# A chain of four transformer blocks on one core: setup as turns beside the first tiles, norms that overlap the last tile's end, one product a scan step, 102-column mixes

## What is computed

```python
# block 0 (8 heads of 32)
x = x + mha(layernorm(x), layernorm(ctx))          # softmax(q k / sqrt(32)) v, then W_o
U = (layernorm(x) @ W_in.T + b_in) @ Bmat          # 64 numbers a row
s = 0
for t in range(1024):                              # a recurrence over the rows
    s = silu(s @ A.T) + U[t]; states[t] = s
x = x + states @ Cmat + (ctxb.mean(axis=1) @ W_prog.T + b_prog)
# block 1 (16 heads of 64), keys and values from layernorm(ctx), causal mask
x = mha(layernorm(x)) @ wo + bo + x
# block 2 (16 heads of 16), mask, then a layernorm over the sum
e = exp(scores - max) * mask; probs = e / (e.sum() + 1e-9)
x = layernorm((probs @ v) @ Wo.T + bo + x) * ln_g + ln_b
# block 3 (16 heads of 16), mask, and an MLP of 1024
x = x + mha(layernorm(x)) @ proj_w + proj_b
x = x + gelu(layernorm(x) @ fc1_w + fc1_b) @ fc2_w + fc2_b
```

## Time and profile before

| | us |
|---|---|
| median of 3 runs | 1478.64 |
| lowest, highest | 1478.23, 1479.79 |
| profiled execution | 1479.49 |
| its span, first to last instruction | 1477.7 |
| TensorE busy, of the span | 1387.4 (94%) |
| VectorE, ScalarE, GpSimd busy | 932.8, 670.1, 559.6 |
| mean granted clock of TensorE | 0.995 of 2.4 GHz |

### The profile page before, as it was taken

One profiled execution on the slowest core, in us unless ns is written; L12 is line 12 of the kernel. 1 busy time (PEld: TensorE's weight loads), 2 busy tenths in 40 slices (PEclk: granted clock), 3 DMA queues, 4 the chain that ended last, 5 costly groups with the idle time before them and its releaser, 6 DMA issues.

```text
span 1477.7 us, 22985 instructions
## 1 busy us (share of the span) xinstructions
PE 1387.4 (94%) x8827; PEld 1147.8 (78%) x8827; DVE 932.8 (63%) x2180; ACT 670.1 (45%) x1483; POOL 559.6 (38%) x699
## 2 busy tenths in 40 slices
PE   6899989999899999999999999989998999899999
PEld 5777777877688678878787887768876887798778
DVE  4677773177755776486757546776577467737771
ACT  3565665513454354534453442335434634453344
POOL 4245342022731463345235411174137314621561
PEclk8999999999999999999999999999999999999999
DMA  4122322020000000000000000000000000000000
GB/s 96 59 61 80 100 94 93 0 84 5 1 8 21 2 2 15 15 1 8 8 15 1 8 16 15 3 1 8 22 1 1 15 15 1 1 15 15 1 1 15
DMA packets 46729, 34.09 MB, mean 23 GB/s; under 512 B 21980, under 2 KB 45339, under 8 KB 46107
## 3 DMA queue, kind: packets, MB, share of 16 engines
q1 hardware_dynamic: 46571, 32.59, 7.8%
q10 hardware_dynamic: 48, 0.01, 0.0%
HBM read 23.26 MB, written 8.39 MB: 21 GB/s over the span
## 4 chain that ended last, share of the span: by engine, by line
PE 76%; DVE 7%; issue 6%; POOL 5%; ACT 3%; DMA 1%; SPq 0%; ACTq 0%; DVEq 0%; POOLq 0%
PE ps L803 11%; PE ps L795 9%; PE ps L755 8%; PE ps L842 8%; PE ps L851 8%; PE ps L774 7%; PE ps L765 6%; PE ps L727 5%; PE ps L811 5%; PE ps L713 4%; PE ps L945 1%; DVE mx L1247 1%; DVE zt L1222 1%; POOL pr L1497 1%; POOL pr L1511 1%
## 5 line engine op out<-in xcount | busy, mean ns | idle before, releaser
L1472 POOL TENSOR_TENSOR rstd<-mv,halfneg 128x1 f32<-128x1 f32 x192 | 106.6, 557 | 501.8 <-DVE mv L1214 500.7
L1511 POOL TENSOR_TENSOR pr<-mx,pr 128x616 f32<-128x616 f32 x128 | 156.2, 1220 | 212.9 <-DVE mx L1247 212.1
L1066 ACT ACTIVATE pr<-pr 128x616 f32<-128x616 f32 x224 | 159.5, 715 | 155.9 <-POOL pr L1511 89.0
L1070 ACT ACTIVATE pr<-ps 128x512 f32<-128x512 f32 x224 | 132.6, 596 | 184.6 <-PE ps L774 183.6
L803 PEld LDWEIGHTS ps<-vtab,pr 128*128 128x128 f32 (+1 forms) x1280 | 165.6, 192 | 21.8 <-ACT pr L1070 17.7
L803 PE MATMUL ps<-vtab,pr 128*128 128x102 f32 (+2 forms) x1280 | 175.3, 285 | 7.0 <-ACT pr L1070 3.5
L1311 DVE TENSOR_TENSOR xt<-xt,ps 128x256 f32<-128x256 f32 x192 | 80.2, 418 | 157.8 <-PE ps L851 70.3
L774 PE MATMUL ps<-ident,pr 128*128 128x128 f32 (+1 forms) x1120 | 160.0, 276 | 13.5 <-POOL pr L1497 5.9
L774 PEld LDWEIGHTS ps<-ident,pr 128*128 128x128 f32 (+1 forms) x1120 | 125.1, 139 | 43.2 <-ACT pr L1066 14.2
L1045 ACT ACTIVATE tt<-ps 128x256 f32<-128x256 f32 x160 | 61.0, 382 | 202.8 <-PE ps L713 202.5
L795 PE MATMUL ps<-vwo,pr 128*128 128x256 f32 (+1 forms) x640 | 149.5, 382 | 1.1 <-ACT pr L1070 0.8
(11 more groups left out here) (198 smaller groups left out, 2406.4 us busy)
## 6 DMA issues: line engine op xcount, KB each, us to landing
out_dram<-xt SPq DMA_DIRECT2D x64, 128.0 KB, 1.7
xt<-in_x_dram SPq DMA_DIRECT2D x32, 128.0 KB, 2.2
xt<-out_dram SPq DMA_DIRECT2D x32, 128.0 KB, 2.1
fc<-in_L_xattn_fc_w_dram SPq DMA_DIRECT2D x2, 1024.0 KB, 7.5
wk<-in_L_xattn_wkv_dram SPq DMA_DIRECT2D x1, 2048.0 KB, 10.0
front<-in_L_xattn_wkv_dram SPq DMA_DIRECT2D x1, 2048.0 KB, 7.7
wo<-in_L_xattn_wo_dram SPq DMA_DIRECT2D x1, 1024.0 KB, 5.2
kb<-in_L_xattn_wq_dram SPq DMA_DIRECT2D x1, 1024.0 KB, 5.0
```

Source lines behind the costliest of these rows:

```text
L1066: ac(v, v, ACT.Exp, scale=-ATTN[key[0]].scale).then_inc(done["expo"], 1)
L1070: ac(pr[:, run.lane, 0:4 * P], bank(run.lane, 0), ACT.Copy).then_inc(done["pturn_main"], 1)
L1472: p.tensor_tensor(rstd[:, lane:lane + 1], mv[:, lane, 1:2], halfneg[:, :], ALU.pow).then_inc(done["rstd"], 1)
L1511: p.tensor_tensor(p8, mx[:, run.lane, :].unsqueeze(2).to_broadcast([P, HG, KEYS]), p8, ALU.subtract).then_inc(done["below"], 1)
```

## The change

It has four parts.

1. **Setup's items are a plan "i"** with turns on every engine, on four banks (4 to 7, of lanes 2 and 3) instead of eight, so that the first tiles' steps stand among them. The query weights come first, then the packed vectors. All `w0` copies are on ScalarE. Six of the twelve DMAs of block 0's values are issued by ScalarE, the others by SyncE. SyncE loads the first tiles of x between the weights, and the fc2 weights wait for the last query of phase 0.
2. **The next tile's start overlaps the last one's end.** In phase 0 its norm stands ahead of the output product, its turn and query after the residual add, its bias before `uproj`; it has buffers of its own (`z0`, `t0`, in the memory of the fc2 weights), statistics of its own, and bank 1. In phase 1 its load, state product (now in bank 1), resume and statistics stand ahead of the last tile's second half of fc2. All strings of `TURNS` are new.
3. **The scan has one product a step.** `sums` holds silu plus `U`; VectorE adds it after each silu (`carry`). `R` becomes two small buffers. `states` and its adds are gone.
4. **Mixes of blocks 2 and 3** stream two copies of three heads, 102 columns instead of 153.

```diff
-COPIES, WCOPY = 3, 160
+COPIES, WCOPY = (3, 2), 160
...
+def lane_steps(lane):
+    first, second = runs_of(lane)[:RUNS], runs_of(lane)[RUNS:]
+    out = [(s, k, first[0]) for s, k in FIRST_NORM + FIRST_QUERY + FIRST_BIAS]
+    for n, run in enumerate(first):
+        follow = first[n + 1:n + 2]
+        out += [(s, k, run) for s, k in FIRST_HEADS]
+        out += [(s, k, f) for f in follow for s, k in FIRST_NORM]
+        out += [(s, k, run) for s, k in FIRST_PROJ]
+        out += [(s, k, f) for f in follow for s, k in FIRST_QUERY]
+        out += [(s, k, run) for s, k in FIRST_STATE]
+        out += [(s, k, f) for f in follow for s, k in FIRST_BIAS]
+        out += [(s, k, run) for s, k in FIRST_U]
+    for n, run in enumerate(second):
+        follow = [] if n + 1 in (RUNS // 2, RUNS) else [second[n + 1]]
+        if n in (0, RUNS // 2):
+            out += [(s, k, run) for s, k in SECOND_GET + SECOND_SSM + SECOND_NORM]
+        out += [(s, k, run) for s, k in SECOND_MAIN]
+        out += [(s, k, f) for f in follow for s, k in SECOND_GET + SECOND_SSM]
+        out += [(s, k, run) for s, k in SECOND_END]
+        out += [(s, k, f) for f in follow for s, k in SECOND_NORM]
+    return out
...
-        steps += [("scan_u", n), ("scan_r", n), ("silu", n)]
+        steps += [("scan_mm", n), ("silu", n), ("carry", n)]
...
+ITEMS = [("w0", i) for i in range(4)] + [("pack", 0)] + [("zT", kc) for kc in range(KC)] + [("w0", 4), ("w0", 5)]
+ITEM_BANKS = (4, 5, 6, 7)
...
             def turn(key, run):
-                        pe.wait_ge(done["u_sb"], at("u_sb", "u", prev(run)))
+                        pe.wait_ge(done["resid"], at("resid", "0", prev(run)))
...
             def scores(key, run):
+                        if run.no > RUNS:
+                            pe.wait_ge(done["resid"], at("resid", "m", prev(run)))
...
+                    if a is L0 and run.no:
+                        pe.wait_ge(done["u_sb"], at("u_sb", "u", prev(run)))
...
-                            dst = o[:, 0:COPIES * WCOPY].rearrange("p (k n) -> p k n", k=COPIES)[:, :, TFIRST[j] * w:(TLAST[j] + 1) * w]
+                            heads = TLAST[j] + 1 - TFIRST[j]
+                            n = COPIES[heads - 2]
+                            dst = o[:, 0:n * WCOPY].rearrange("p (k n) -> p k n", k=n)[:, :, TFIRST[j] * w:(TLAST[j] + 1) * w]
...
             def ssm(key, run):
+                elif is_first(run):
                     pe.wait_ge(done["resid"], at("resid", "m", prev(run)))
+                else:
+                    pe.wait_ge(done["gelu"], at("gelu", "mb", prev(run)))
...
-            def scan_r(n, run):
-                if n:
-                    pe.wait_ge(done["silu"], at("silu", n - 1))
-                mm(scan_out(n), aT[:, :], chunk_view(R[:, :, 0:S])[:, :, :, n % CH], start=False, stop=True,
-                   skip_group_check=True).then_inc(done["scan_r"], 1)
+            def scan_mm(n, run):
...
+                else:
+                    pe.wait_ge(done["carry"], at("carry", n - 1))
+                src = sums if n else U
+                mm(scan_out(n), aT[:, :], chunk_view(src[:, :, 0:S])[:, :, :, n % CH], start=True, stop=True).then_inc(done["scan_mm"], 1)
...
+            def v0_lay(key, run):
+                set_up(act, ("v0", BATCH - 1))
+                act.wait_ge(v0_zero, 1)
+                lay_values(act, L0, vtmp0, vtab["0"], laid["0"], 1)
...
+            def carry(n, run):
+                dve.wait_ge(done["silu"], at("silu", n))
+                v.tensor_tensor(chunk_view(sums[:, :, 1:S + 1])[:, :, :, n % CH], R[:, n % 2, :, 1:NCH + 1],
+                                chunk_view(U[:, :, 1:S + 1])[:, :, :, n % CH], ALU.add).then_inc(done["carry"], 1)
...
-            def states(q, run):
-                own = slice(1 + q * S // PIECES, 1 + (q + 1) * S // PIECES)
-                v.tensor_tensor(R[:, :, own], R[:, :, own], U[:, :, own], ALU.add).then_inc(done["states"], 1)
```

More of the change, by code:

```diff
@@ L119, in table_steps @@
+SECOND_END = [("fc2", "mb"), ("resid", "m"), ("store", "x")]
 def table_steps(pair):
     p = str(pair)
[L122 removed]
+    steps = [] if pair else ([("v0_put", p)] + [("weights_get", i) for i in range(LOADS - 1)] + [("wkv1_get", p), ("masks", "2"), ("weights_get", LOADS - 1)])
     if pair == 0:
@@ L173 @@
-PLANS = {str(lane): [(s, k, run) for run in runs_of(lane) for s, k in (AFTER if run.phase else BEFORE)] for lane in range(LANES)}
+    return steps + [("gap", 0), ("gap_turn", 0), ("agree", 0), ("more_pe", 0), ("more_act", 0)]
+ITEMS = [("w0", i) for i in range(4)] + [("pack", 0)] + [("zT", kc) for kc in range(KC)] + [("w0", 4), ("w0", 5)]
+ITEMS += [("k0", c) for c in range(KC)] + [("v0", b) for b in range(BATCH)]
+ITEMS += [("w0", 6), ("w0", 7), ("wprog", 0), ("a", 0), ("wU", 0), ("mean", 0)]
@@ new lines @@
+MADE_BY = {
+    "tensor": ("item_mm", "turn", "query", "scores", "pturn", "mix", "proj", "uproj", "ssm", "fc1", "fc2",
+               "w2_mm", "wqt_mm", "k_mm", "wk_mm", "vt_mm", "vwo_mm", "v_mm", "scan_mm", "gap_turn", "more_pe"),
+    "scalar": ("item_act", "v0_lay", "turned", "query_bias", "expo", "pturn_main", "u_sb", "gelu", "w2_sb", "wqt_sb", "k1_sb", "vt_sb", "silu", "more_act"),
+    "vector": ("ctx_stats", "ctx_norm", "item_dve", "stats", "aggr", "norm", "bound", "rowmax", "shift", "rowsum", "den_eps", "recip", "weigh",
+               "pturn_rest", "heads", "resid", "resume", "wk_sb", "vwo_sb", "k_sb", "v_sb", "carry", "ends", "gap", "agree"),
+    "gpsimd": ("ctx_rstd", "head_masks", "row_masks", "value_zero", "zeros", "rstd", "prebias", "keep", "below", "maskmul", "gain", "offset", "masks", "fold", "vtw_zero"),
+    "sync": ("load", "put", "get", "store", "weights_get", "wkv1_get", "v0_put", "v_lay")}
@@ L592, in weights_get @@
                 dst, src, signal = LATE[i]
+                if i == LOADS - 1:
+                    sp.wait_ge(done["query"], max(at("query", "0", r) for r in last_runs(0, 1)))
                 sp.dma_start(dst, src).then_inc(signal, 16)
@@ L833, in ssm @@
                 at_t = 1 + run.tile * P
-                mm(bank(lane, 0)[:, 0:H], R[:, run.batch % PAIR, at_t:at_t + P], cmat[:, pair, :],
+                mm(bank(lane, 1)[:, 0:H], sums[:, run.batch % PAIR, at_t:at_t + P], cmat[:, pair, :],
                    start=True, stop=True).then_inc(done["ssm"], 1)
@@ L1316, in resume @@
                 xs = x[:, slot(run), :]
-                v.tensor_tensor(xs, xs, bank(run.lane, 0)[:, 0:H], ALU.add).then_inc(done["resume"], 1)
+                v.tensor_tensor(xs, xs, bank(run.lane, 1)[:, 0:H], ALU.add).then_inc(done["resume"], 1)
             def wk_sb(key, run):
```

477 lines of the change are left out of this document (257 added, 220 removed).

## The result

The changed kernel takes **1444.38 us** (median of 4 runs, 1442.48 to 1445.57), the kernel before 1479.22 on the same chip (4 runs, 1478.23 to 1481.86): a ratio of 0.9754, 95% interval 0.9739 to 0.9769 (the quotient of the two medians, 0.9764, lies inside it), or 35 us less. The forecast was 1432, range 1403 to 1460. The profiled execution took 1445.13 us with a span of 1443.4 (1479.5 and 1477.7 before).

What follows compares the result with a forecast made beforehand. TensorE's work was taken to bound phase 1, but not phase 0, where it idles 22 us. Terms -10 - 3 - 17 - 9 - 8 = -47 from the profiled 1479.5 us, less 0.85, gave 1432 us, range 1403 to 1460.

Steps and rivals of the forecast that it cites:

- the likeliest case: Whole kernel: the forecast of 1432 us, its case 1418 to 1443 by itself, chance 0.55.
- Mixes: Blocks 2 and 3, in phase 1: 102-column mixes take 1.11 us each; -10 us, ends -19 and -5.
- Setup: Start of kernel: first tiles' work fills waits, ScalarE is held 5.2 us by six copies; -3 us, +3 to -9.
- Phase 0: 46 to 242 us: the next tile's norm and query leave each lane's chain; -17 us, ends 0 and -28.
- Scan and tables: First state read 61 us after first silu, remaining tables fill the scan's gaps; -9 us, between -15 and +5.
- Phase 1 overlap: Phase 1: state product, resume and statistics run beside the last tile's fc2; -8 us, ends 0 and -25.
- the sign I had named: Phase 1: if the forecast is right, TensorE's idle time is lower by a third.
- a granted clock of 0.50 anywhere but in setup: Outside setup: the clock at its 1.2 GHz level there would show the forecast wrong.
- Removed work alone: Whole kernel: only removed work counts, overlap merely moves waits; 1455 us, chance 0.22.
- the reordering does nothing in phase 0 and a step is 2 us: Phase 0 and scan: no gain from reordering, scan +5 us; about 1466 us, chance 0.05.
- Blocked norms: Lanes' norms, stretched by GpSimd's adds, hold the chains; slower, 1493 us at a mean of 0.8 us, chance 0.04.
- All it can: Whole kernel: the overlap gives all it can, phase 0 -26 and phase 1 -20 us; 1403 us, chance 0.14.

Runs made afterwards that it cites:

- Kept warm: The changed kernel with 24 products of unused result on TensorE ahead of the item that waits 5.31 us for ScalarE: 1437.79 us, ratio 0.9707.
- the pair that differs in phase 0 alone: Changed kernel with setup items as a block and all value copies on SyncE, phase 0 in new or old order: ratios 0.9712 and 0.9821 to the kernel before.

## Why the prediction was right, and where it was wrong

The time lies in the range and the likeliest case was the right one, 12 us too low. Two terms erred by +10 and +6 us and one by -4, so that the total is nearer than its parts.

- **Mixes**, -10: -7 to -9. The price of 1.11 was right (1.105). The mean over all mixes fell less, 1.323 to 1.259 us, since many wait inside; that cover was taken too thin. The rule of the Trainium skill that would have given -15 ("TensorE: Matmul & The Clock Gate", section LDWEIGHTS) is not quite borne out here: ten records took 1.105 us, not 1.07.
- **Setup**, -3 (+3 to -9): +7.4 at the first u. *This step failed.* "I take -3, from +3 (the 5.2 us shown in full) to -9" priced ScalarE's hold right (5.19 us) but took it for the worst case. It left out that TensorE, idle for 5.31 us, then runs 13.6 us at the lower level; the text called that clock "open" and gave it no price. Kept warm, the first u comes 5.3 us earlier; with the hold gone too, 9.4. Without both, setup is -2.0 (49.23 for 51.25), near the -3 forecast. A smaller part: the 308-column products of L730 took 4.33 us where those of before took 2.31 (from 14.58 us on). They now come at 12.45 us, and TensorE runs at half its pace up to 16.5 us, where before it did up to 13.9; that is in every version with the early start.
- **Phase 0**, -17: -10.8, and -13 in every trace without the changed kernel's own dip to 0.50 at 183.9 us (190.8 to 178). The mechanism held, forecast 179 us and 180.0 measured from first to last u; but I had set 179 against 196 us, a stretch that began at 46 us, 5 us ahead of the first u. The term was mis-sized by that comparison. Some of it is also paid back ahead of the first u, where the second tiles' starts now stand: 8.8 us were left at the last u in the pair that differs in phase 0 alone. With GpSimd's adds gone it was 175.4.
- **Scan and tables**, -9: -9.4 from last u to the 46th exponential. Steps were 1.47 us, not 1.57: the add takes 0.38 as assumed, but the silu only 0.28, presumably since it now writes adjacent columns (0.38 in the earlier trace rows). Blocks of tables took that back: one interval is 6.94 us, and all tables together add some 10 us to the 31 intervals where 7 were counted. The state read comes 60 us after the first silu, as said; there the two errors cancel, which is luck. From the state read to the 46th exponential 11 us came out (67.2 for 78.3), where -14.7 + 4 were counted.

```profile
241.29 0.28 ACT L1236 ACTIVATE zt<-ps 128x128 f32<-128x128 f32 x1
241.60 0.38 DVE L1472 TENSOR_TENSOR scan<-zt,scan 128x128 f32<-128x128 f32 x1 [5.38 <-ACT zt L1236]
242.03 0.68 PE L1045 MATMUL ps<-scan,aT 128*128 128x128 f32 x2 [0.19 <-DVE scan L1472]
242.75 0.28 ACT L1236 ACTIVATE zt<-ps 128x128 f32<-128x128 f32 x1 [1.19 <-PE ps L1045]
...
259.30 5.63 ACT L1224 ACTIVATE front<-ps,cols 64x154 f32<-64x154 f32 x14
264.95 0.28 ACT L1236 ACTIVATE zt<-ps 128x128 f32<-128x128 f32 x1
...
301.25 0.46 PE L919 MATMUL ps<-cmat,scan 128*128 128x256 f32 x1 [1.82 <-ACTq L1249]
```

- **Phase 1 overlap**, -8: -12.3, half as much again. "Less than half of the 18 can come out" was argued from 49 us of idle TensorE, but idle time fell only from 19.4 to 15.7 us in 375 to 840: the sign I had named, a third less, did not come, while 88 more instructions were done (27 of them owing to the shorter mixes: with 153 columns they are 2,892). Modelled ends show waits as busy time, so idle TensorE was no ceiling. Two thirds came out.
- **The clock.** "The granted clock is 1.00 everywhere but in setup" was misread from the rounding of the earlier trace rows: the kernel before has a stretch at 0.50 in phase 1.

```profile
1259.80:1263.20 3.40, 3.40 (x17) 3.40 (x16) 1.52 (x4) 0.72 (x1) 2.07 (x3) 0.50 0.00 0
```

So the sign of being wrong "a granted clock of 0.50 anywhere but in setup" came (at 183.9 and 1235 us) and says little by itself.
- **Rivals.** Removed work alone (1455) falls: the overlaps gave 9 to 13 us in phase 0 and 12.3 in phase 1. That the reordering does nothing in phase 0 and a step is 2 us (1466) falls with it, and with steps of 1.47. Blocked norms fall: means of 475 and 536 ns, far from 730. The effect itself is there, smaller: 0.41 us with a quiet GpSimd. The lock that the Trainium skill describes ("SBUF — State Buffer", section SBUF: two separate sides) would fit that; that a norm takes that port pair, no run here shows. "All it can" (1403) falls, though the copies on SyncE lead over a quarter of the way there.

The sum was -47, and the kernel with the copies on SyncE has a span 46.8 us below that of before. That is partly luck (phase 1 offsets phase 0). Of the 12.5 us of span between it and the changed kernel, 9.4 are in setup and have one origin, the copies on ScalarE: 4.2 by the hold and 5.3 by the clock after TensorE's wait. 2.0 are phase 0's stretch at 0.50, whose cause is not shown, and 1.1 lie in phase 1.

## What to carry to other kernels

A DMA issued from a computing engine costs that engine its time, 0.87 us each here, and what pays for it can be another engine's clock: price both, and put such issues on a queue where nothing waits. A long idle stretch of TensorE can cost itself and then the slower work after it; if the wait can't go, useless products in it can pay (5.3 us here), but try it: ahead of the kernel's first item they brought 2.4 us by the ratio and 0.8 in the trace. When an overlap is judged, count instructions done per stretch and not idle time, and measure both terms between the same two events.
